# Routed experts in blocks of two halves of 64 rows, and two blocks at a time on TensorE

## The chip, the cores and the metric

The kernel runs on one core of a Trainium2 chip. The metric is the device time of one execution in microseconds (us), lower is better.

## The reference

The input `x` is 16 x 256 tokens of 256 values. It goes through two gated layers:

```
x = x + tanh(g_xattn) * cosine(LN(x) Wv^T + bv, ctx Wt^T + bt)      # attention part, per batch 256 x 256
h = LN(x)                                                           # 4096 tokens, D = 256
shared = (silu(h @ w1) * (h @ w2)) @ w3                             # one shared expert, hidden width 1024
scores = sigmoid(h @ router_w)                                      # 16 experts
top2   = top_k(scores + expert_bias, 2); gates = scores at those two, else 0
routed = sum over e of gates[:, e] * ((silu(h @ W1[e]) * (h @ W2[e])) @ W3[e])   # hidden width 256
x = x + tanh(g_ffn) * (shared + routed)
```

Each token uses two of sixteen experts, so there are 8192 routed rows. The kernel computes only those rows; how many fall to each expert is known only at run time.

## The kernel before

All five engines have a program of their own, written out by hand, and wait for each other on semaphores. The order of the work on an engine is the order of its program.

- **Attention part and router** (0 to about 118 us): eight chunks of 512 tokens. `router` (L1306) already uses strips of the array: four groups of 128 tokens go to four strips of 32 columns, `tile_position=(0, 32 * i)`, each with its own moving operand. Ahead of it on TensorE stand matmuls of line L1254 (128 elements, all 128 columns), behind it those of L1264.
- **Shared expert**, first part: steps of one chunk and one eighth of the hidden width (`hidden`, L1385, and `shared_rows`, L1406). Weights and activations are kept as sums of two f16 parts (hi and lo), so every product is three f16 matmuls: hi*hi, hi*lo, lo*hi. During these steps VectorE computes the routing, GpSimd scatters the token numbers into a table of slots, and ScalarE and VectorE cast the routed weights into `WR` (hi by L713, lo by L1076), half an expert at a time, as the list `CUTS` says per step.
- **Routed experts** (277.56 to 465.15 us): `NRUN` blocks of 128 rows. Every expert's rows are rounded up to 128, so a block belongs to one expert. Its number comes from a packed word (`blk_word`), four blocks to a word.
- **The rest of the shared expert**, in which GpSimd gathers the routed rows back (L561) and VectorE adds them (L1052); then the stores.

One routed block b goes through these steps:

1. GpSimd fetches its 128 rows by an indirect DMA into one of four slots (`fetch`, L544).
2. TensorE transposes them (`block_transpose`, L1457, two f32 transposes), into bank 2; ScalarE writes the hi part to `XTB` (`x_hi`, L749), VectorE the lo part (`x_lo`, L1131).
3. TensorE computes both hidden products (`block_hidden`, L1468, 6 matmuls of 512 elements, the weights are the moving operand).
4. ScalarE takes the silu (`r_silu`, L756), VectorE multiplies (`gated`, L1138).
5. TensorE transposes the result (`hidden_transpose`, L1477, bank 3); `g_hi` (L762) and `g_lo` (L1143) write `GT`.
6. TensorE computes the rows (`block_rows`, L1488, 6 matmuls of 256 elements, bank 4); VectorE copies them out (`rows`, L1150), SyncE stores them (`store_block`, L432).

TensorE's loop runs per b: hidden product of b, transpose of the gated part of b - 1, transpose of the rows of b + 2, rows product of b - 2. `XTB`, `GT`, `SIL`, `G` have two buffers each. `experts` reads the packed word into registers, and `weights` forms the address in `WR` from them at run time.

The functions that the diff touches:

Of the kernel before, what the change touches and what calls it, by code (L numbers as in the profile page):

```python
# [19 lines left out]
P = 128  # L20


def flamingo_block(nc, x, x_t, ctx_t, g_xattn, g_ffn, wv_t, bv, wt_t, bt, router_w, expert_bias,
# [21 lines left out]
    NRUN = (2 * TOK + E * (P - 1)) // P  # L45
    NBLK = -(-NRUN // 8) * 8
    WE = 2 * KD * RH + (RH // P) * D
# [20 lines left out]
    with ctx:  # L68
# [19 lines left out]
        XTB = sb("XTB", [P, 2, 2, KD, P], F16)  # L88
# [31 lines left out]
        blk_word = sb("blk_word", [1, NBLK // 4], I32)  # L120
        row_iota = sb("row_iota", [P, 1], F32)
        pack = sb("pack", [P, NBLK // 4], F32)
# [7 lines left out]
        def arena(shape):  # L130
# [27 lines left out]
        BV4 = XTB[:, :, :, :, :].rearrange("p a b k n -> p (a b k n)").bitcast(F32).rearrange("p (i h) -> p i h", i=TPC)  # L158
# [5 lines left out]
            .rearrange("p (a k n) -> p a k n", a=2, k=KD)  # L164

# [38 lines left out]
        ended = sb("ended", [P, E], F32)  # L204
        bef = sb("bef", [P, 1], F32)
# [4 lines left out]
        SHARED_ROWS = (bank[3], bank[4])  # L210

# [89 lines left out]
        w_lo = sem("w_lo")  # L301

# [38 lines left out]
        CUTS = [0] * (J + 2) + [2, 1, 1] * 6 + [1] * 8  # L341
# [3 lines left out]
        assert sum(TILES.values()) == NT  # L345

# [4 lines left out]
        def _(sp):  # L351
# [81 lines left out]

            with sp.Fori(0, NBLK // 4 - 1) as i:
                for u in range(4):
                    store_block(i, u)
            for b in range(NBLK - 4, NRUN):
                store_block(b // 4, b % 4)
# [18 lines left out]
        def _(pool):  # L457
# [12 lines left out]
            pool.iota(row_iota[:, :], pattern=[[0, 1]], base=0, channel_multiplier=1,  # L470
                      allow_small_or_imprecise_dtypes=True)
            pool.memset(pack[:, :], 0.0).then_inc(c_mem, 1)
            for k in range(6):

                pool.wait_ge(c_mem, 3 + k)
                pool.affine_select(out=pack[:, :], in_=pack[:, :], compare_op=ALU.not_equal, fill=float(E ** k),
                                   base=2 - k, pattern=[[-4, NBLK // 4]], channel_multiplier=1).then_inc(c_mem, 1)
# [93 lines left out]
        def _(act):  # L571
# [173 lines left out]
            def x_hi(b, u, first=False):  # L745
                act.wait_ge(b_tx, b + 1)
                if not first:
                    act.wait_ge(b_h, b - 1)
                act.activation(XTB[:, u, 0], bank[2][:, 0:KD * P].rearrange("p (k n) -> p k n", k=KD), ACT.Copy)\  # L749
                    .then_inc(b_xhi, 1)  # L750
# [7 lines left out]
            def g_hi(b, u, first=False):  # L758
# [3 lines left out]
                act.activation(GT[:, u, 0], bank[3][:, 0:RH].rearrange("p (k n) -> p k n", k=RH // P), ACT.Copy)\  # L762
                    .then_inc(b_ghi, 1)

            act.wait_ge(s_g, NSE)
            x_hi(0, 0, True)
            x_hi(1, 1, True)
            for b in range(NRUN):
                r_silu(b, b % 2, b < 2)
                if b >= 1:  # L770
                    g_hi(b - 1, (b - 1) % 2, b - 1 < 2)
                if b + 2 < NRUN:
                    x_hi(b + 2, b % 2)
            g_hi(NRUN - 1, (NRUN - 1) % 2)
# [20 lines left out]
        def _(dve):  # L795
# [190 lines left out]
            def sum_experts(inc):  # L986

                link(dve.tensor_scalar(ni[:, :], inc[:, PADT + NT - 1, :], float(P - 1), None, ALU.add))
                link(dve.tensor_scalar(bi[:, :], ni[:, :], 7, None, ALU.arith_shift_right))
# [11 lines left out]
                link(dve.tensor_scalar(base_row[:, :], nf[:, :], float(P), None, ALU.mult))  # L1001
# [21 lines left out]
            def block_experts(ends):  # L1023

                link(dve.tensor_scalar(ended[:, :], ends, row_iota[:, :], None, ALU.is_le))
                link(dve.tensor_reduce(bef[:, :], ended[:, :], AX.X, ALU.add))
                dve.tensor_scalar(bef[:, :], bef[:, :], float(E - 1), None, ALU.min).then_inc(bef_ready, 1)

            def block_words():
                dve.wait_ge(word_mm, 1)  # L1030
                dve.tensor_copy(blk_word[:, :], bank[6][0:1, 0:NBLK // 4]).then_inc(routed_ok, 1)
# [97 lines left out]
            def x_lo(b, u):  # L1129
                dve.wait_ge(b_xhi, b + 1)  # L1130
                dve.tensor_tensor(XTB[:, u, 1], bank[2][:, 0:KD * P].rearrange("p (k n) -> p k n", k=KD),  # L1131
                                  XTB[:, u, 0], ALU.subtract).then_inc(b_xlo, 1)

# [7 lines left out]
            def g_lo(b, u):  # L1141
                dve.wait_ge(b_ghi, b + 1)
                dve.tensor_tensor(GT[:, u, 1], bank[3][:, 0:RH].rearrange("p (k n) -> p k n", k=RH // P),  # L1143
                                  GT[:, u, 0], ALU.subtract).then_inc(b_glo, 1)

            def rows(b, i, u, first=False):
                dve.wait_ge(b_y, b + 1)
                if not first:
                    dve.wait_ge(st_y[u], i * 16)
                dve.tensor_copy(YS[:, u, :], bank[4][:, 0:D]).then_inc(b_yev, 1)  # L1150

            x_lo(0, 0)
            x_lo(1, 1)
            add_shared(NCA, steps=EX)
            for b in range(NRUN):
                gated(b, b % 2, b < 2)
                if b >= 1:
                    g_lo(b - 1, (b - 1) % 2)
                if b + 2 < NRUN:
                    x_lo(b + 2, b % 2)  # L1160
                if b >= 2:
                    rows(b - 2, (b - 2) // 4, (b - 2) % 4, b < 6)
            g_lo(NRUN - 1, (NRUN - 1) % 2)
            rows(NRUN - 2, (NRUN - 2) // 4, (NRUN - 2) % 4)

            dve.wait_ge(b_tg, NRUN)
            gate_hidden(NSE, NSE % J)
            hidden_lo(NSE, NSE % J)
            rows(NRUN - 1, (NRUN - 1) // 4, (NRUN - 1) % 4)


# [32 lines left out]
        def _(pe):  # L1204
# [162 lines left out]
            def words():  # L1367

                pe.wait_ge(bef_ready, 1)
                pe.matmul(bank[6][0:1, 0:NBLK // 4], bef[0:NBLK, :], pack[0:NBLK, :], start=True, stop=True)\  # L1370
                    .then_inc(word_mm, 1)
# [70 lines left out]

            def experts(i):
# [109 lines left out]
```

## Time and profile before

| | |
|---|---|
| device time, median of 3 runs | 597.67 us (597.29 to 598.88) |
| the profiled execution's own time | 600.83 us |
| its span, first to last instruction | 598.7 us |
| granted TensorE clock over the span | 0.971 |
| instructions | 11199 |
| blocks of the routed part | 79 |

In the rows further down, PE is TensorE's matmuls, PEld its weight loads (they run beside matmuls), DVE is VectorE, ACT ScalarE, POOL GpSimd, SPq the queue of SyncE. `PE bank L1468 x6` in a chain is six matmuls of line 1468. A duration of a matmul includes a fixed latency that overlaps the next one, so a stream's pace is read from starts. A row of a group has its busy time, the mean of one in ns, and the idle time of its engine ahead of it.

### The profile page before, as it was taken

The numbers are of one execution on the slowest core, as the hardware profiler recorded it, in microseconds if no ns is written. First come the engines' busy times: TensorE is split into PE (matmuls) and PEld (weight loads), VectorE is DVE, ScalarE is ACT, GpSimd is POOL, SyncE is SP. The second block draws the span as 40 slices with busy tenths as digits, with TensorE's granted clock in tenths as the row PEclk, the third lists the DMA queues.
The fourth block names the chain that finished last, engine by engine and source line by source line (L and its number), as shares of the span: only waits on it lengthen the run. The fifth ranks groups of instructions, "written<-read, shape, count | busy, mean of one in ns | idle before, by whom it ended". The sixth has DMA issues, their size and how long they took to land.

```text
span 598.7 us, 11199 instructions
## 1 busy us (share of the span) xinstructions
PE 550.9 (92%) x3410; PEld 351.6 (59%) x3410; DVE 362.7 (61%) x845; ACT 243.5 (41%) x541; POOL 273.7 (46%) x264
## 2 busy tenths in 40 slices
PE   4899899889899999598999999999999989879797
PEld 2567676555555566255666666666666555445454
DVE  2426887777877675356556556655665456454755
ACT  3435666652265554244343334333433323222322
POOL 3002675434387877733334333433340255637560
PEclk9879999999999999889999999999999999979899
DMA  8999353356151110021333333333442133624342
GB/s 236 316 376 358 125 175 142 142 194 211 36 159 36 55 37 0 2 73 37 111 114 111 107 113 117 109 107 110 111 111 78 54 108 86 193 72 133 99 138 71
DMA packets 54561, 74.25 MB, mean 124 GB/s; under 512 B 8256, under 2 KB 44544, under 8 KB 54512
## 3 DMA queue, kind: packets, MB, share of 16 engines
q1 hardware_dynamic: 44992, 52.67, 26.7%
q0 software_dynamic: 8944, 18.83, 11.9%
q10 hardware_dynamic: 576, 2.10, 1.1%
q8 instruction: 31, 0.51, 0.4%
q14 instruction: 18, 0.15, 0.1%
HBM read 50.56 MB, written 23.01 MB: 123 GB/s over the span
## 4 chain that ended last, share of the span: by engine, by line
PE 73%; DVE 11%; issue 6%; DMA 3%; POOL 3%; SPq 2%; ACT 2%; DVEq 0%; POOLq 0%; ACTq 0%
PE bank L1385 22%; PE bank L1468 17%; PE bank L1406 12%; PE bank L1488 9%; PE bank L1477 3%; PE bank L1457 3%; DMA WR<-in_ctx_t 2%; PE bank L1223 2%; POOL X L495 1%; PE bank L1250 1%; DVE STAGE L870 1%; DVE GS L1068 1%; DVE X L1040 1%; DMA xrow<-STAGE 1%; PE bank L1212 1%
## 5 line engine op out<-in xcount | busy, mean ns | idle before, releaser
L1385 PE MATMUL bank<-XTC,WS 128*128 128x512 f16 x768 | 180.3, 384 | 0.6 <-issue 0.5
L544 POOL DMA_INDIRECT ROWS<-xrow,idx x79 | 76.2, 964 | 118.9 <-PE bank L1457 113.8
L1385 PEld LDWEIGHTS bank<-XTC,WS 128*128 128x128 f16 x768 | 76.0, 99 | 81.8 <-issue 7.4
L1406 PE MATMUL bank<-WS,GS 128*128 128x256 f16 x768 | 98.5, 280 | 25.6 <-DVE GS L1068 14.0
L1468 PE MATMUL bank<-WR,XTB 128*128 x474 | 115.3, 379 | 0.6 <-issue 0.6
L1406 PEld LDWEIGHTS bank<-WS,GS 128*128 128x128 f16 x768 | 74.6, 100 | 53.8 <-DVE GS L1068 20.4
L561 POOL DMA_INDIRECT ROWS<-yrow,posi x64 | 65.4, 1021 | 67.4 <-DVE X L1052 29.6
L1062 DVE SCALAR_TENSOR_TENSOR G<-bank,SIL 128x512 f32<-128x512 f32 x63 | 43.5, 690 | 77.7 <-ACT SIL L698 57.4
L527 POOL DMA_INDIRECT slot_token<-tokid,sloti x64 | 74.6, 1165 | 23.6 <-issue 19.2
L698 ACT ACTIVATE SIL<-bank 128x512 f32<-128x512 f32 x63 | 37.6, 596 | 110.8 <-PE bank L1385 77.0
L1138 DVE SCALAR_TENSOR_TENSOR G<-bank,SIL 128x256 f32<-128x256 f32 x79 | 33.6, 425 | 76.0 <-ACT SIL L756 75.9
L756 ACT ACTIVATE SIL<-bank 128x256 f32<-128x256 f32 x79 | 30.3, 383 | 114.5 <-PE bank L1468 113.7
L1468 PEld LDWEIGHTS bank<-WR,XTB 128*128 128x128 f16 x474 | 46.2, 98 | 40.8 <-issue 2.0
L705 ACT ACTIVATE GS<-G 128x512 f16<-128x512 f32 x63 | 39.7, 630 | 63.3 <-DVE G L1062 52.7
L1488 PE MATMUL bank<-WR,GT 128*128 x474 | 64.7, 273 | 0.0
L495 POOL TENSOR_TENSOR X<-X,WR 128x512 f32 (+1 forms) x16 | 23.6, 1495 | 67.1 <-DVE WR L840 67.1
L1068 DVE TENSOR_TENSOR GS<-G,GS 128x512 f16<-128x512 f32 x56 | 38.8, 693 | 20.9 <-ACT GS L705 14.6
L1488 PEld LDWEIGHTS bank<-WR,GT 128*128 128x128 f16 x474 | 46.4, 98 | 4.7
L1143 DVE TENSOR_TENSOR GT<-bank,GT 128x256 f16<-128x256 f32 x79 | 32.8, 415 | 2.6 <-ACT GT L762 2.6
L1131 DVE TENSOR_TENSOR XTB<-bank,XTB 128x256 f16<-128x256 f32 x79 | 32.8, 415 | 1.0 <-ACT XTB L749 1.0
L1150 DVE COPY ROWS<-bank 128x256 f32<-128x256 f32 x79 | 32.8, 415 | 0.7 <-PE bank L1488 0.7
L749 ACT ACTIVATE XTB<-bank 128x256 f16<-128x256 f32 x79 | 30.9, 392 | 1.6 <-PE bank L1457 1.6
(156 smaller groups left out, 631.7 us busy)
## 6 DMA issues: line engine op xcount, KB each, us to landing
yrow<-ROWS SPq DMA_DIRECT2D x79, 128.0 KB
WR<-in_routed_w SPq DMA_DIRECT2D x39, 256.0 KB, 5.7
X<-in_x SPq DMA_DIRECT2D x4, 1024.0 KB, 12.6
xrow<-STAGE SPq DMA_DIRECT2D x8, 512.0 KB, 2.9
xtd<-STAGE SPq DMA_DIRECT2D x8, 512.0 KB, 2.6
out<-X SPq DMA_DIRECT2D x7, 512.0 KB
WR<-in_ctx_t SPq DMA_DIRECT2D x4, 768.0 KB, 10.2
WR<-in_shared_w SPq DMA_DIRECT2D x3, 1024.0 KB, 14.5
```

Of the source, the lines that this page charges most:

```text
L527: pool.indirect_dma_start(out=slot_token, in_=tokid[:, t:t + 1], in_offset=None, out_offset=bass.IndirectOffsetOnAxis(ap=sloti[:, k, t:t + ...
L544: pool.indirect_dma_start(out=XG[:, u, :], out_offset=None, in_=xrow, in_offset=bass.IndirectOffsetOnAxis(ap=idx[:, b:b + 1].bitcast(U32), ...
L561: pool.indirect_dma_start(out=YG[:, u, k, :], out_offset=None, in_=yrow, in_offset=bass.IndirectOffsetOnAxis(ap=posi[:, k, t:t + 1].bitcas ...
L698: act.activation(SIL[:, a, :], HIDDEN[a][0][:, :], ACT.Silu, scale=1.0 / WSCALE).then_inc(s_sil, 1)
L705: act.activation(GS[:, a, 0, :], G[:, a, :], ACT.Copy).then_inc(s_ghi, 1)
L1062: dve.scalar_tensor_tensor(out=G[:, a, :], in0=HIDDEN[a][1][:, :], scalar=1.0 / WSCALE, in1=SIL[:, a, :], op0=ALU.mult, op1=ALU.mult).then ...
L1068: dve.tensor_tensor(GS[:, a, 1, :], G[:, a, :], GS[:, a, 0, :], ALU.subtract).then_inc(s_glo, 1)
L1138: dve.scalar_tensor_tensor(out=G[:, u, 0:RH], in0=bank[u][:, RH:2 * RH], scalar=1.0 / WSCALE, in1=SIL[:, u, 0:RH], op0=ALU.mult, op1=ALU.m ...
L1385: last = pe.matmul(acc[:, :], WS[:, wx, at:at + P], XTC[:, u, xx, k, :], start=(k == 0 and m == 0), stop=(k == KD - 1 and m == 2))
L1406: last = pe.matmul(acc, GS[:, a, gx, i * P:(i + 1) * P], WS[:, wx, at:at + D], start=(n in (NSE, n - j) and m == 0 and i % 2 == 0), stop=( ...
L1468: last = pe.matmul(bank[u][:, :], XTB[:, u, xx, k, :], w, start=(k == 0 and m == 0), stop=(k == KD - 1 and m == 2))
L1488: last = pe.matmul(bank[4][:, 0:D], GT[:, u, gx, k, :], w, start=(k == 0 and m == 0), stop=(k == RH // P - 1 and m == 2))
```

## The change

- The rows of an expert are rounded up to 64 (`PR`), no longer to 128. A block is two halves of 64 rows that may belong to two experts. `NRUN` goes from 79 to 72, `NBLK` from 80 to 72. There is a packed word for the even halves and one for the odd ones.
- Each matmul of a block becomes two, for rows 0 to 63 and 64 to 127, on columns 0 to 63 and 64 to 127 of the array and of the output's partitions. Each first loads the 64 rows of its half into its columns of the array (a PEld instruction) and then streams its own expert's weights past them.
- TensorE reads the even half's weights from `WR` at a run-time address, as before. The odd half's are copied to fixed places `W12` and `W3` (in the staging buffer, two sets), w1 and w2 by VectorE (`odd_first`), w3 by ScalarE (`odd_second`); both read the expert's number from the packed word themselves.
- TensorE's loop takes two blocks at a time: both hidden products, both rows products of the pair before, then all transposes. Banks 5, 6 and 7 double those of the transposes and of the rows; `XTB` has four buffers.
- The casts of the weights end one step earlier.

```diff
-    NRUN = (2 * TOK + E * (P - 1)) // P
+    PARTS = 2
+    PR = P // PARTS
+    NRUN = -(-((2 * TOK + E * (PR - 1)) // PR) // PARTS)
+    NRUN += NRUN % 2
     NBLK = -(-NRUN // 8) * 8
+    NW = NBLK // 4
...
-        XTB = sb("XTB", [P, 2, 2, KD, P], F16)
+        XTB = sb("XTB", [P, 4, 2, KD, P], F16)
...
+        stage_h = stage_f.bitcast(F16)
+        W12 = stage_h[:, 0:4 * W3E].rearrange("p (u h n) -> p u h n", u=2, h=2)
+        W3 = stage_h[:, 4 * W3E:4 * WE].rearrange("p (u h n) -> p u h n", u=2, h=2)
...
+        XB = (bank[2], bank[5])
+        GB = (bank[3], bank[6])
+        YB = (bank[4], bank[7])
...
-        CUTS = [0] * (J + 2) + [2, 1, 1] * 6 + [1] * 8
+        CUTS = [0] * (J + 2) + [2, 1, 1] * 7 + [1] * 4 + [0]
...
+        def odd_half(w, b):
+            e = (w >> (4 * (b % 4 + 2))) & (E - 1)
+            return WR[:, :].rearrange("p (e h n) -> p e h n", e=E, h=2)[:, ds(e, 1), :, :]\
+                .rearrange("p a h n -> p (a h) n")
...
# ScalarE
+            def odd_second(b, w, first=False):
+                if not first:
+                    act.wait_ge(b_y, b - 1)
+                act.activation(W3[:, b % 2], odd_half(w, b)[:, :, W3E:WE], ACT.Copy).then_inc(odd_w3, 1)
...
+            for b in range(0, NRUN, 2):
+                r_silu(b, 0, b == 0)
+                r_silu(b + 1, 1, b == 0)
+                if b == 0:
+                    x_hi(2)
+                    x_hi(3)
+                if b % 4 == 0:
+                    w = act.value_load(blk_word[0:1, ds(NW + b // 4, 1)])
+                odd_second(b, w, b == 0)
+                g_hi(b, 0, b == 0)
+                g_hi(b + 1, 1, b == 0)
+                if b + 4 < NRUN:
+                    x_hi(b + 4)
+                    x_hi(b + 5)
+                odd_second(b + 1, w, b == 0)
...
# VectorE
-                link(dve.tensor_scalar(ended[:, :], ends, row_iota[:, :], None, ALU.is_le))
+                for s in range(PARTS):
+                    last = dve.tensor_scalar(ended[:, s, :], ends, row_iota[:, s:s + 1], None, ALU.is_le)
+                link(last)
...
+            def odd_first(b, w, first=False):
+                if not first:
+                    dve.wait_ge(b_h, b - 1)
+                dve.tensor_copy(W12[:, b % 2], odd_half(w, b)[:, :, 0:W3E]).then_inc(odd_w12, 1)
...
+            for b in range(0, NRUN, 2):
                 if b + 2 < NRUN:
+                    if (b + 2) % 4 == 0:
+                        w = dve.value_load(blk_word[0:1, ds(NW + (b + 2) // 4, 1)])
+                    odd_first(b + 2, w)
+                gated(b, 0, b == 0)
+                gated(b + 1, 1, b == 0)
+                if b + 2 < NRUN:
+                    odd_first(b + 3, w)
+                if b == 0:
+                    x_lo(2)
+                    x_lo(3)
+                else:
+                    rows(b - 2)
+                    rows(b - 1)
+                g_lo(b, 0)
+                g_lo(b + 1, 1)
+                if b + 4 < NRUN:
+                    x_lo(b + 4)
+                    x_lo(b + 5)
...
# TensorE, block_hidden (block_rows in the same way, with W3 and odd_w3)
+                pe.wait_ge(odd_w12, b + 1)
...
                 for k in range(KD):
-                    hi = weights(e, k * 2 * RH, 2 * RH)
-                    lo = weights(e, WE + k * 2 * RH, 2 * RH)
+                    at = k * 2 * RH
+                    hi = weights(e, at, 2 * RH), W12[:, u, 0, at:at + 2 * RH]
+                    lo = weights(e, WE + at, 2 * RH), W12[:, u, 1, at:at + 2 * RH]
                     for m, (xx, w) in enumerate(((0, hi), (0, lo), (1, hi))):
-                        last = pe.matmul(bank[u][:, :], XTB[:, u, xx, k, :], w,
-                                         start=(k == 0 and m == 0), stop=(k == KD - 1 and m == 2))
+                        for s in range(PARTS):
+                            part = slice(s * PR, (s + 1) * PR)
+                            last = pe.matmul(bank[u][part, :], XTB[:, b % 4, xx, k, part], w[s],
+                                             start=(k == 0 and m == 0), stop=(k == KD - 1 and m == 2),
+                                             tile_position=(0, s * PR))
...
-            for b in range(NRUN):
+            for b in range(0, NRUN, 2):
                 if b % 4 == 0:
                     es = experts(b // 4)
-                block_hidden(b, b % 2, es[b % 4 + 2], b < 2)
-                if b == 1:
+                block_hidden(b, es[b % 4 + 2])
+                block_hidden(b + 1, es[b % 4 + 3])
+                if b == 0:
+                    block_transpose(2)
+                    block_transpose(3)
                     pe.wait_ge(s_base, NCA + 1)
-                if b >= 1:
-                    hidden_transpose(b - 1, (b - 1) % 2, b == 1)
-                if b + 2 < NRUN:
-                    block_transpose(b + 2, (b + 2) % 4, 16 * ((b + 2) // 4 + 1))
-                if b >= 2:
-                    block_rows(b - 2, b % 2, es[b % 4], b == 2)
+                else:
+                    block_rows(b - 2, es[b % 4])
+                    block_rows(b - 1, es[b % 4 + 1])
+                hidden_transpose(b)
+                hidden_transpose(b + 1)
+                if b + 4 < NRUN:
+                    block_transpose(b + 4)
+                    block_transpose(b + 5)

             hidden(NSE, NCA % 2, EX)
-            hidden_transpose(NRUN - 1, (NRUN - 1) % 2)
-            block_rows(NRUN - 2, (NRUN - 2) % 2, es[NRUN - 2 - (NBLK - 6)])
+            block_rows(NRUN - 2, es[NRUN - 2 - LAST_WORD])
             hidden(NSE + 1, NCA % 2, EX + 1)
-            block_rows(NRUN - 1, (NRUN - 1) % 2, es[NRUN - 1 - (NBLK - 6)])
+            block_rows(NRUN - 1, es[NRUN - 1 - LAST_WORD])
```

## Rows read from the trace of the kernel before

**Rows 1.** The page: busy time per engine, and the chain that ended last.
```profile
PE 550.9 (92%) x3410; PEld 351.6 (59%) x3410; DVE 362.7 (61%) x845; ACT 243.5 (41%) x541; POOL 273.7 (46%) x264
...
PE 73%; DVE 11%; issue 6%; DMA 3%; POOL 3%; SPq 2%; ACT 2%; DVEq 0%; POOLq 0%; ACTq 0%
```

**Rows 2.** Stretches: from:to, length, busy per engine, granted clock, DMA share, GB/s.
```profile
277.56:465.15 187.59, 187.54 (x1247) 127.95 (x1248) 111.63 (x315) 73.12 (x234) 70.18 (x74) 1.00 0.36 107
```

**Rows 3.** The chain in order of time (start, us, what): first, steady and last blocks.
```profile
277.56 1.51 PE bank L1468 x6
...
455.95 1.30 PE bank L1468 x6
457.25 0.22 PE bank L1477 x2
457.47 0.22 PE bank L1457 x2
457.68 0.66 PE bank L1488 x6
458.34 1.29 PE bank L1468 x6
...
462.89 1.38 PE bank L1468 x6
...
465.15 0.86 PE bank L1385 x4
```

**Rows 4.** The timeline of ScalarE and VectorE in one steady block (start, us, what).
```profile
455.65 0.41 DVE L1143 TENSOR_TENSOR GT<-bank,GT 128x256 f16<-128x256 f32 x1
455.99 0.42 DVE L1131 TENSOR_TENSOR XTB<-bank,XTB 128x256 f16<-128x256 f32 x1
...
457.28 0.38 ACT L756 ACTIVATE SIL<-bank 128x256 f32<-128x256 f32 x1 [1.45 <-PE bank L1468]
457.56 0.38 ACT L762 ACTIVATE GT<-bank 128x256 f16<-128x256 f32 x1
```

**Rows 5.** The timeline of TensorE around one chunk's router.
```profile
77.03 1.05 PE L1254 MATMUL bank<-GS,XTB 128*128 128x128 f32 x8
78.02 0.65 PE L1306 MATMUL bank<-STAGE,rw 128*32 128x128 f32 x16
78.59 1.16 PE L1264 MATMUL bank<-ident,rt 128*128 128x128 f32 x8
```

**Rows 6.** Groups by form: TensorE's matmuls of L1254 and three weight loads.
```profile
L1254 PE MATMUL bank<-GS,XTB 128*128 128x128 f32 x64 | 9.0, 287 | 0.0
...
L1306 PEld LDWEIGHTS bank<-STAGE,rw 128*32 128x32 f32 x128 | 3.0, 109 | 3.0 <-DVE WR L840 1.5 <-issue 0.8
...
L1264 PEld LDWEIGHTS bank<-ident,rt 128*128 128x128 f32 x64 | 7.7, 189 | 1.2 <-issue 1.2
...
L1468 PEld LDWEIGHTS bank<-WR,XTB 128*128 128x128 f16 x474 | 46.2, 98 | 40.8 <-issue 2.0
```

**Rows 7.** Groups by form: VectorE, one long form and three TENSOR_SCALAR forms.
```profile
L1076 DVE SCALAR_TENSOR_TENSOR WR<-STAGE,WR 128x768 f16<-128x768 f32 x6 | 5.8, 959 | 0.2
...
L870 DVE TENSOR_SCALAR STAGE<-X,mv,rs 128x256 f32 x20 | 6.9, 409 | 1.2 <-DMA xrow<-STAGE 0.7
...
L815 DVE TENSOR_SCALAR gsum<-gsum 128x24 f32<-128x24 f32 x1 | 0.2, 178 | 0.0
...
L815 DVE TENSOR_SCALAR gsum<-gsum 128x8 f32<-128x8 f32 x1 | 0.2, 172 | 0.0
```

**Rows 8.** Groups by form: ScalarE's cast of half an expert.
```profile
L713 ACT ACTIVATE WR<-WR 128x768 f16<-128x768 f32 x26 | 20.9, 827 | 0.0
```

**Rows 9.** Groups: GpSimd's fetches of routed rows.
```profile
L544 POOL DMA_INDIRECT ROWS<-xrow,idx x79 | 76.2, 964 | 118.9 <-PE bank L1457 113.8 <-issue 3.2 <-DMA idx<-slot_token 1.8
```

**Rows 10.** The chain at 246 us; DMA queues from 280 to 460 (packets, MB, share).
```profile
246.67 5.91 issue
...
q8 instruction: 13, 0.21, 0.5%
```

More of the change, by code:

```diff
@@ L1154, in _ @@
+            odd_first(0, w, True)
+            x_lo(1)
+            odd_first(1, w, True)
             add_shared(NCA, steps=EX)
[L1155 to L1158, printed above, removed]
+            for b in range(0, NRUN, 2):
                 if b + 2 < NRUN:
-                    x_lo(b + 2, b % 2)
-                if b >= 2:
-                    rows(b - 2, (b - 2) // 4, (b - 2) % 4, b < 6)
-            g_lo(NRUN - 1, (NRUN - 1) % 2)
@@ L1450, in weights, with block_transpose @@
                     .rearrange("p a n -> p (a n)")
-            def block_transpose(b, slot, count):
-                pe.wait_ge(xg[slot], count)
-                if not (isinstance(b, int) and b == 0):
-                    pe.wait_ge(b_xlo, b)
+            def block_transpose(b):
+                slot = b % 4
+                pe.wait_ge(xg[slot], 16 * (b // 4 + 1))
+                if b >= 2:
+                    pe.wait_ge(b_xlo, b - 1)
                 for k in range(KD):
-                    last = pe.transpose(bank[2][:, k * P:(k + 1) * P], XG[:, slot, k * P:(k + 1) * P], ident[:, :])
+                    last = pe.transpose(XB[b % 2][:, k * P:(k + 1) * P], XG[:, slot, k * P:(k + 1) * P], ident[:, :])
@@ L1470, in block_hidden, with hidden_transpose @@
                 last.then_inc(b_h, 1)
-            def hidden_transpose(b, u, first=False):
+            def hidden_transpose(b):
                 pe.wait_ge(b_g, b + 1)
-                if not first:
-                    pe.wait_ge(b_glo, b)
+                if b >= 2:
+                    pe.wait_ge(b_glo, b - 1)
                 for k in range(RH // P):
-                    last = pe.transpose(bank[3][:, k * P:(k + 1) * P], G[:, u, k * P:(k + 1) * P], ident[:, :])
+                    last = pe.transpose(GB[b % 2][:, k * P:(k + 1) * P], G[:, b % 2, k * P:(k + 1) * P], ident[:, :])
@@ L1487, in block_rows @@
                     for m, (gx, w) in enumerate(((0, hi), (0, lo), (1, hi))):
-                        last = pe.matmul(bank[4][:, 0:D], GT[:, u, gx, k, :], w,
-                                         start=(k == 0 and m == 0), stop=(k == RH // P - 1 and m == 2))
+                        for s in range(PARTS):
+                            part = slice(s * PR, (s + 1) * PR)
+                            last = pe.matmul(YB[u][part, 0:D], GT[:, u, gx, k, part], w[s],
+                                             start=(k == 0 and m == 0), stop=(k == RH // P - 1 and m == 2),
+                                             tile_position=(0, s * PR))
```

110 lines of the change are left out of this document (58 added, 52 removed).

## The prediction

> **What bounds the kernel now.** I read the page's busy shares first: TensorE is busy for 92% of the span, and the chain that ended last runs through it for 73% [rows 1]. Then the stretches: the diff works on the one from the first block's first matmul (277.56) to the first matmul behind the last block (465.15), and there TensorE is busy for 187.54 of 187.59 us, VectorE for 111.6, ScalarE for 73.1 and GpSimd for 70.2, at a granted clock of 1.00 [rows 2]. Last the chain inside it: one block is hidden 1.29-1.30, transposes of G 0.22, transposes of X 0.22, row products 0.66, and the next block starts 2.39 us after the last one, with no wait between [rows 3]. Of the 79 blocks, 78 starts are (462.89 - 277.56)/78 = 2.38 us apart. So the stage is 79 blocks of TensorE work, and all else is hidden.
>
> **The change part by part.**
>
> *Fewer blocks.* 2 x 4096 routed rows padded to 64 per expert fill at most (8192 + 16 x 63)/64 = 143 halves, so 72 blocks in place of 79.
>
> *The products of a block.* Each product becomes two, on 64 columns of the array each: the hidden part issues 12 matmuls and 12 loads for 6, the rows part the same. If two halves stream side by side, the time stays at 1.29 and 0.66. The trace has such tiles: the router issues 16 matmuls of 128 elements on four strips of 32 columns, and the next group starts 0.57 us after it; the 8 untiled ones of the same size ahead of it take 0.99 up to it [rows 5]. With starts (1.05 - 0.287)/7 = 0.109 apart [rows 5, 6], 16 in series would be 1.74. So strips do overlap, four-fold, and 16 matmuls with 16 loads are issued in under 0.6 us; this block needs 24 and 24 in 1.95. I take full overlap. The bound from above is none at all: + 1.95 per block.
>
> *The price of going into tiles and out.* 8 x 0.109 = 0.87 of the 0.99 is streaming, 0.12 is left going in; 4 x 0.109 = 0.44 of the 0.57, 0.13 is left coming out [rows 5]. The new order puts H(b) H(b+1) R(b-2) R(b-1) on tiles and four transposes after them, so each pair of blocks pays one way in and one out: 0.25 us. Bounds: 0 (if the router's gaps are its own waits) and twice that.
> The Trainium skill, TensorEngine Tiling (Array Packing), § Key Properties, says that changing the tiling mode drains TensorE; it agrees with these gaps, and is the rule that speaks against the change: without it the sum below would be 9 us better.
>
> *Loads of weights.* A load of 32 f32 columns takes 109 ns, of 128 f32 189, of 128 f16 98 [rows 6]; from the first two, 0.83 ns per f32 column. Two loads of 64 columns per 107 to 109 ns of the rows part are then about 107, just hidden; the router sustains four of 32 in the same time [rows 5]. I take nothing. Bound from above: both loads in the open at 109 each, + 0.11 for each of 6 pairs, + 0.65 per block.
> The Trainium skill, same page, § Restrictions, has column tiling turn off Fast Weight Load; the 98 ns of the f16 load against 189 for f32 would be that fast form, and the sum would move only if the slower load came out from under 107 ns.
>
> *Copies of the odd expert's weights.* VectorE gains one copy of 2 x 1024 f16 per block, ScalarE one of 2 x 512. ScalarE: 768 elements took 827 ns, so 1024 take at most 1.10 us [rows 8]. Now 0.28 from start to start of its ops of 256 [rows 4]: a pair is 6 x 0.28 + 2 x 1.1 = 3.9 of 5.0 us, hidden. VectorE: its ops of 256 start 0.34 apart [rows 4], eight a pair, 2.72 us. The copy isn't in the trace. At one element per cycle it is 0.96 us for 768 plus 1280 x 1.04 ns = 2.29 us [rows 7] (the same form as the 409 ns of a TENSOR_SCALAR of 256). But the same TENSOR_SCALAR with a plain constant goes from 172 to 178 ns between 8 and 24 f32 elements, 0.4 ns for one, where one per cycle would be 17 ns more: two f32 per cycle, 8 bytes [rows 7]. At 8 bytes per cycle 2048 f16 are 512 cycles: 0.53 + 0.16 = 0.69 us. Between 0.69 and 2.29 I take 0.69, since a copy has no per-partition scalar, as the fast rows haven't. Then VectorE has 2.72 + 2 x 0.62 = 3.96 of 5.0 us. It decides once a copy takes over (5.03 - 2.72)/2 = 1.15 us.
> The Trainium skill, VectorE: DVE Perf Modes, § The perf-mode tier table, gives a bf16 copy of 2048 in SBUF 693 ns; no copy here shows it.
>
> *The order within a pair.* The waits that could bite: the copy odd_first(b+2) waits for H(b), and gated(b), both rows, both g_lo and both x_lo are queued behind it on VectorE. Followed through with T = 5.03 from the pair's start: H(b) done and seen at 1.63, odd_first to 2.3, gated(b) to 2.7; silu(b+1) to 3.3, gated(b+1) to 3.75, while the transpose of G(b+1) starts at 4.4: 0.6 spare. odd_first(b+3) to 4.4, rows to 5.0, g_lo to 5.7 (they follow ScalarE's g_hi, which waits for R(b-2) and its own copy, to 5.15), x_lo to 6.35, and the next odd_first is not due before 6.66: 0.3 spare. R(b) at T + 2.7 finds g_lo(b) 2 us old. So nothing but TensorE sets the pace. GpSimd's fetches, 0.96 each [rows 9], two in 5.0 us, are as hidden as now; the four slots and the distance in blocks are the same. Register loads of the packed word stand on ScalarE and VectorE every fourth block, inside those 0.3 and 0.6.
>
> *Ends of the stage.* The first pair has no rows products and must wait for gated(1): about 4.5 us. Then 33 pairs of 4.77 + 0.25 = 5.03 and two without X transposes of 4.59: 175.2. Sum 179.7 against 187.59: - 7.9. Behind it the tail has three more changes of tiling (+ 0.4) and one transpose pair less (- 0.2).
>
> *The rest.* One more compare, one more matmul of 18 columns, a 10% smaller table: under 0.3 us, beside the shared steps. The casts come half a step earlier, beside TensorE; the last step has none, so the first x_lo comes perhaps 0.5 us earlier; TensorE waits there for the packed word anyway: 0. After the stage all is as before, 7.7 us sooner.
> What I can't price is fetching of instructions: at 246.67 the chain has 5.91 us in which TensorE waits for nothing shown, and TensorE gets 24 instructions more a block. In the stage itself 13 instruction packets went by without such a gap [rows 10]. I take 0, and 5 us to either side, because the fetches fall at other places now.
>
> Sum for the profiled execution: its span 598.7 and 2.1 around it are 600.8; 600.8 - 7.7 = 593.1. That execution is 3.2 above the median of 597.67, so against the median: **590.0 us**.
>
> **The rivals.**
> *A, no gap at the tiles' borders, or instruction gaps that vanish.* 36 x 0.25 = 9 us less: 581. For it: the router's gaps may be its waits. Against: both times are alike to 0.01 us.
> *B, near 597: the gain eaten.* Gaps of double size (+ 9) or a VectorE copy at 1.22 us (two elements a cycle: 2.72 + 2 x 1.14 = 5.0, no slack left, each late silu shows). 595 to 600.
> *C, VectorE becomes the bound by the port that it shares with GpSimd* (slower). If a copy stands still while GpSimd writes out a fetch of 0.96 us, a pair is 2.72 + 2 x (0.62 + 0.96) = 5.9: 35 x 0.85 = + 30, so 619. For it: two fetches and two copies in each pair. Against: fetches start when the X transposes end (4.6 to 6.5), copies run from 1.6 and from 3.7; little of them meets. It decides from 0.5 us of hold-up per copy.
> The Trainium skill, SBUF — State Buffer, § Who interferes with whom, has a Vector op in a 2-port mode and GpSimd lock each other out for the whole instruction; no row here has the two together.
> *D, the copy at one element per cycle.* 2.72 + 2 x 2.2 = 7.1: + 73, so 663. For it the 409 ns row, against it the 172 and 178.
> *E, halves or loads do not overlap.* Loads in the open 0.65 x 72 = + 47, 637; nothing overlapping 1.95 x 72 = + 140, 730. Against: the router.
> *That the change does not do what it says* can't be on the count: 72 is fixed when it is built.
>
> **How the numbers follow.** About 0.3% (1.8 us) can be told from no change. Forecast 0.50 (its own range 585 to 595), A 0.10, B 0.14, C 0.14, D 0.06, E 0.06. Faster: forecast 0.49, A 0.10, B 0.03: 0.62. Same: B 0.08 and the forecast's edge 0.01: 0.09. Slower: B 0.03, C, D, E: 0.29. The range goes from A's 581 to part of C, 615; D, E and the worse half of C (0.19) are left out.
>
> **What would show it.** Hidden groups still 1.3 us for 12 matmuls; a pair of blocks 5.0 us, with two gaps of 0.12 to 0.13 around the transposes; the copy at 0.7 us; VectorE under 85% busy in the stage; ScalarE's copies at 1.0 to 1.1. Wrong would be waits on VectorE's G or on a copy in the chain (C, D), or groups of 12 that take 2.6 us (E).

## The result, and the profile after

The changed kernel takes 592.69 us (median of 4, 591.55 to 593.16) against 597.94 us (median of 4): a ratio of 0.9908, 95% interval 0.9887 to 0.9929, so 5.3 us less. Forecast were 590.0 us, with 585 to 595 as the forecast's own range. Its profiled execution took 592.25 us with a span of 590.5.

The page of the changed kernel, answering to [rows 1]:

```profile
PE 545.1 (92%) x4164; PEld 348.4 (59%) x4164; DVE 397.0 (67%) x890; ACT 305.8 (52%) x592; POOL 273.5 (46%) x257
...
PE 68%; DVE 13%; issue 8%; DMA 3%; POOL 3%; ACT 2%; another core or an unknown queue 2%; SPq 1%; DVEq 0%; POOLq 0%; ACTq 0%
```

Its stretches, answering to [rows 2]: the routed stage from the first block's first matmul to the first shared step behind it.

```profile
275.78:459.56 183.78, 181.66 (x1990) 124.45 (x1990) 145.80 (x358) 134.66 (x285) 69.81 (x67) 1.00 0.35 99
```

TensorE is still busy nearly all the time, at a clock of 1.00. VectorE went from 111.6 to 145.8 us, ScalarE from 73.1 to 134.7. The chain of a steady pair of blocks, answering to [rows 3] (L1537 is the hidden product, L1563 the rows, L1547 and L1521 the transposes of G and of X):

```profile
409.95 2.71 PE bank L1537 x24
412.66 1.31 PE bank L1563 x24
413.97 0.59 PE bank L1547 x4
414.56 0.44 PE bank L1521 x4
415.00 2.71 PE bank L1537 x24
```

24 hidden matmuls take 2.71 us and 24 rows matmuls 1.31; 12 and 12 full-width ones take 2.59 and 1.31 (the run without tiles below). So two halves stream side by side. A pair takes 5.04 to 5.05 us. Of the 0.27 above 4.77, 0.12 stands at the first hidden product (2.71 less 2.59) and 0.15 at the first transpose (0.59 less 0.44), where TensorE enters and leaves the tiles. The groups by form, answering to [rows 6 to 9]:

```profile
L563 POOL DMA_INDIRECT ROWS<-xrow,idx x72 | 76.0, 1055 | 105.8 <-PE bank L1521 92.7 <-issue 11.3 <-DMA idx<-slot_token 1.9
L788 ACT ACTIVATE STAGE<-WR 128x1024 f16 x72 | 76.8, 1066 | 10.7 <-PE bank L1563 10.1 <-issue 0.6
L1194 DVE COPY STAGE<-WR 128x2048 f16 x72 | 49.6, 689 | 17.6 <-PE bank L1537 12.6 <-issue 5.0
L1563 PEld LDWEIGHTS bank<-WR,GT 128*64 128x64 f16 x432 | 47.1, 110 | 7.9 <-issue 0.8
```

VectorE's copy takes 689 ns, ScalarE's 1066, a load of 64 columns 110, and a fetch of GpSimd now 1055 where it was 964.

**Where the 8.2 us between the two spans lie.** Same places in both chains:

| from, to | before | after | difference |
|---|---|---|---|
| start, first hidden product of the shared expert that is in the chain | 118.06 | 121.30 | +3.2 |
| ... start of the last shared rows ahead of the stage | 157.09 | 152.85 | -4.2 |
| ... first block | 2.41 | 1.63 | -0.8 |
| the routed stage | 187.59 | 183.78 | -3.8 |
| ... shared rows again | 7.22 | 7.36 | +0.1 |
| ... end | 126.33 | 123.58 | -2.8 |

The routed stage gives 3.8, not 7.9. The other large terms belong to stretches that the diff hardly touches; the experiments below say which of them are real. TensorE's very first hidden matmul of the shared expert comes earlier than the one in the chain, at 109.7 us before and 112.9 after; the text below calls it the first hidden step, and it moved by the same 3.2 us.

### The profile page after: what moved, and what is told of

Read it like the earlier page. It is cut to its first block, busy times and chain, and to the rows that moved or that the text cites. A ratio compares the mean times of both kernels' runs of the same rounds, so it can differ in the third digit from the quotient of the medians.

```text
span 590.5 us, 13102 instructions
## 1 busy us (share of the span) xinstructions
PE 545.1 (92%) x4164; PEld 348.4 (59%) x4164; DVE 397.0 (67%) x890; ACT 305.8 (52%) x592; POOL 273.5 (46%) x257
## 4 chain that ended last, share of the span: by engine, by line
PE 68%; DVE 13%; issue 8%; DMA 3%; POOL 3%; ACT 2%; another core or an unknown queue 2%; SPq 1%; DVEq 0%; POOLq 0%; ACTq 0%
PE bank L1446 18%; PE bank L1537 16%; PE bank L1467 10%; PE bank L1563 8%; PE bank L1547 3%; PE bank L1282 3%; PE bank L1521 3%; DVE X L1077 2%; DVE G L1099 2%; DMA WR<-in_ctx_t 2%; POOL X L514 2%; PE bank L1271 1%; PE bank L1309 1%; DVE GS L1105 1%
## 5 line engine op out<-in xcount | busy, mean ns | idle before, releaser
L563 POOL DMA_INDIRECT ROWS<-xrow,idx x72 | 76.0, 1055 | 105.8 <-PE bank L1521 92.7
L1467 PE MATMUL bank<-WS,GS 128*128 128x256 f16 x768 | 95.8, 275 | 22.4 <-DVE GS L1105 15.0
L1537 PE MATMUL bank<-WR,XTB 128*64 x432 | 100.1, 381 | 1.1 <-issue 0.9
L1537 PE MATMUL bank<-STAGE,XTB 128*64 128x512 f16 x432 | 100.2, 381 | 0.0
L788 ACT ACTIVATE STAGE<-WR 128x1024 f16 x72 | 76.8, 1066 | 10.7 <-PE bank L1563 10.1
L1537 PEld LDWEIGHTS bank<-WR,XTB 128*64 128x64 f16 x432 | 45.7, 109 | 42.8 <-issue 8.0
L1194 DVE COPY STAGE<-WR 128x2048 f16 x72 | 49.6, 689 | 17.6 <-PE bank L1537 12.6
L1563 PE MATMUL bank<-STAGE,GT 128*64 128x256 f16 x432 | 53.3, 273 | 0.0
L1563 PE MATMUL bank<-WR,GT 128*64 x432 | 53.3, 273 | 0.0
L1563 PEld LDWEIGHTS bank<-WR,GT 128*64 128x64 f16 x432 | 47.1, 110 | 7.9 <-issue 0.8
L1563 PEld LDWEIGHTS bank<-STAGE,GT 128*64 128x64 f16 x432 | 47.1, 110 | 0.0
```

The lines of the kernel that those rows point to most:

```text
L563: pool.indirect_dma_start(out=XG[:, u, :], out_offset=None, in_=xrow, in_offset=bass.IndirectOffsetOnAxis(ap=idx[:, b:b + 1].bitcast(U32), ...
L788: act.activation(W3[:, b % 2], odd_half(w, b)[:, :, W3E:WE], ACT.Copy).then_inc(odd_w3, 1)
L1194: dve.tensor_copy(W12[:, b % 2], odd_half(w, b)[:, :, 0:W3E]).then_inc(odd_w12, 1)
L1467: last = pe.matmul(acc, GS[:, a, gx, i * P:(i + 1) * P], WS[:, wx, at:at + D], start=(n in (NSE, n - j) and m == 0 and i % 2 == 0), stop=( ...
L1537: last = pe.matmul(bank[u][part, :], XTB[:, b % 4, xx, k, part], w[s], start=(k == 0 and m == 0), stop=(k == KD - 1 and m == 2), tile_posi ...
L1563: last = pe.matmul(YB[u][part, 0:D], GT[:, u, gx, k, part], w[s], start=(k == 0 and m == 0), stop=(k == RH // P - 1 and m == 2), tile_posi ...
```

## The experiments

The experiments were made in four series, and the kernel before takes another time in each: 575.5 us in the first (below: the quiet series), 615.9 in the second, 622.5 in the third, 637.3 in the fourth. The first and third have the same chip number, and so have the second and fourth, so the chip alone isn't shown to make the difference. In the last three series the times of one kernel spread too far for their totals to decide anything, and traces are compared. The routed stage is steadier: 187.47 to 187.59 us in the traces of the kernel before, 181.95 to 183.78 in those of the changed one.

**The changed kernel again.**

> The changed kernel once more, for a second trace of it. Theory (TensorE sets the pace of the pairs; what lies outside the routed stage varies from one execution to the next): 592.7 within 1, pairs again 5.04 to 5.06 us, stage 183.8 within 0.5; the stretch from 237 to 274 us, where the chain has gaps that nothing explains, may differ by several us. Rival (those gaps belong to the program): they stand at the same places with the same sizes within 1 us.

572.22 us (median of 10) against 575.53: ratio 0.9945, interval 0.9912 to 0.9978, so 3.3 us less. The stage is 181.95 us. The chain in the stretch of the scatters, in order of time:

```profile
241.95 1.31 PE bank L1467 x12
243.26 2.59 PE bank L1446 x12
245.85 1.31 PE bank L1467 x12
```

Steps of 3.90 without a gap, where both kernels had gaps of several us in the first comparison ([rows 10] for before). So the gaps aren't fixed by the program; what sets them is open. From the first hidden step to the routed stage the changed kernel takes 156.9 us here, 162.9 in the first comparison and 194.9 in the third series. Of the forecast for this run the total and the length of the stage (183.8 expected) were off; the pairs held, and the rival on the gaps is out. The stage came out 1.8 us shorter than in the first comparison.

**One more way out of the tiles and in.**

> The transposes of one block's rows move in between the two hidden products of the pair: the same instructions, but TensorE leaves and enters the 64-column tiles twice in a pair and not once. Theory (each way out and in costs 0.27 us together, as the traces show it): 34 pairs x 0.27 = 9 us more than the changed kernel, about 602, pairs of 5.3. Rival (the 0.27 is the latency of the transposes' own waits, not of the change of tiles): within 2 us of the changed kernel, 593.

```diff
                 block_hidden(b, es[b % 4 + 2])
+                if b >= 2 and b + 4 < NRUN:
+                    block_transpose(b + 4)
                 block_hidden(b + 1, es[b % 4 + 3])
...
                 if b + 4 < NRUN:
-                    block_transpose(b + 4)
+                    if b == 0:
+                        block_transpose(b + 4)
                     block_transpose(b + 5)
```

587.64 us, 15.4 more than the changed kernel in the same series (572.22); forecast were 9. The chain of one pair:

```profile
305.05 1.42 PE bank L1537 x12
306.47 0.39 PE bank L1521 x2
306.86 0.01 issue
306.87 1.49 PE bank L1537 x12
308.36 1.31 PE bank L1563 x24
309.67 0.59 PE bank L1547 x4
310.25 0.22 PE bank L1521 x2
```

A pair is 5.42 us, 0.38 more and not 0.27: two transposes between tiles take 0.39 where they are 0.22 among others, and the tiles are entered again for 0.20. So the border's price is real, and dearer around a short visit. 33 pairs at + 0.38 are 12.5 us of the stage's + 13.0 (194.97 against 181.95). One pair took 5.7 us: its moved transposes (415.27) waited for VectorE's `x_lo`, at the end of a chain that begins with a copy of ScalarE. Another 1.7 us of the 15.4 are in front of the stage, where this program's first hidden step comes at 114.6 us and not at 112.9. In the pair shown nothing waits at either border, so the rival (waits of the transposes) is out.

**No tiles.**

> Every block is multiplied at full width with the even half's expert alone: 6 and 6 matmuls on all 128 columns, no tiles. The copies of the odd expert's weights are still made and waited for, but not used, so the odd expert's products are left out. Theory (halves stream side by side at no cost, only the borders cost): pairs of 4.77 to 4.80 us, so 35 x 0.27 = 9.5 us less than the changed kernel, 583. Rival 1 (the loads of the halves or their streams cost as well): more than 12 us less. Rival 2 (VectorE or ScalarE is the bound as it stands, the copies hide the borders): pairs stay near 5.0, 592.

```diff
-                        for s in range(PARTS):
-                            part = slice(s * PR, (s + 1) * PR)
-                            last = pe.matmul(bank[u][part, :], XTB[:, b % 4, xx, k, part], w[s], ..., tile_position=(0, s * PR))
+                        last = pe.matmul(bank[u][:, :], XTB[:, b % 4, xx, k, :], w[0], ...)
```

562.08 us, 10.1 less than the changed kernel; the stage is 173.18 against 181.95. The chain:

```profile
341.14 2.59 PE bank L1535 x12
343.73 1.31 PE bank L1558 x12
345.04 0.44 PE bank L1544 x4
345.47 0.44 PE bank L1521 x4
345.91 2.59 PE bank L1535 x12
```

4.77 us a pair, to the hundredth what was computed from the kernel before. In a steady pair the halves cost 0.27 us and nothing else: neither loads nor streams show.

**No copies.**

> The copies of the odd expert's weights are made for the first two blocks only, so later odd halves use those weights; every matmul and every other wait stays. Theory (the copies are hidden, but for some 1.3 us at the stage's start where VectorE's chain of x_lo, copy, add, copy, gate stands on the path): 591 to 592, pairs 5.04, and GpSimd's fetches back from 1.06 to 0.96 us each if the copies hold it up through a shared port. Rival (the pace of the pairs is set by VectorE's copies or ScalarE's, with TensorE's gaps of 0.12 and 0.15 being waits for them): pairs of 4.8, 583.

```diff
-                dve.tensor_copy(W12[:, b % 2], odd_half(w, b)[:, :, 0:W3E]).then_inc(odd_w12, 1)
+                if b < 2:
+                    dve.tensor_copy(W12[:, b % 2], odd_half(w, b)[:, :, 0:W3E]).then_inc(odd_w12, 1)
...
# ScalarE's copy and TensorE's waits for both copies in the same way
```

570.69 us (median of 10), 1.5 less; the intervals of both against before overlap (0.9893 to 0.9956, and 0.9912 to 0.9978). The trace decides: pairs still 5.04 to 5.05, the stage 181.47. In the pairs the copies are hidden. At the stage's start they cost 0.47 us, not the 1.3 that was expected: the second pair begins 5.74 us behind the first, and 6.21 behind it in the changed kernel. GpSimd's fetches:

```profile
L563 POOL DMA_INDIRECT ROWS<-xrow,idx x72 | 69.3, 963 | 103.6 <-PE bank L1523 90.7 <-issue 11.3 <-DMA idx<-slot_token 1.6
```

963 ns without copies, 1093 in the changed kernel of the same series. This run takes away the copies of both engines; a steady pair of the changed kernel tells whose it is:

```profile
301.34 0.95 POOL L563 DMA_INDIRECT ROWS<-xrow,idx  x1 [2.57 <-PE bank L1521]
301.91 1.08 ACT L788 ACTIVATE STAGE<-WR 128x1024 f16 x1
302.60 1.22 POOL L563 DMA_INDIRECT ROWS<-xrow,idx  x1 [0.30 <-issue]
303.01 0.69 DVE L1194 COPY STAGE<-WR 128x2048 f16 x1 [0.35 <-PE bank L1537]
```

The fetch beside ScalarE's copy takes 0.95 us as ever, the one beside VectorE's takes 1.22. Over the stage, 35 fetches that run beside a copy of VectorE last 1199 ns in the mean, and the 32 others, all beside a copy of ScalarE, 954. VectorE's copy began in the middle of the fetch and took its usual time (694 ns in the mean beside a fetch, 684 without). So the two run at the same time, GpSimd loses some 0.25 us by it, and it has the time.

**Each copy twice.**

> VectorE makes each of its copies of the odd expert's weights twice. Theory (VectorE has 2.72 us of other starts per pair and 0.62 for a copy, TensorE 5.05): VectorE then needs 2.72 + 4 x 0.62 = 5.2, and more with its waits for the first copy's end, so it becomes the bound: pairs of 5.3 to 5.8, 9 to 26 us more than the changed kernel, 602 to 619. Rival (VectorE still has more slack than that sum says): within 2 us of 593.

Chain of this kernel, two starts of the first copy of a pair (the rows between are VectorE's and its sequencer's):

```profile
400.00 0.62 DVE STAGE L1194
...
405.31 0.62 DVE STAGE L1194
```

A pair is 5.31 us in the mean, VectorE's sum 5.2 without its waits for each first copy to end; the stage takes 193.01. So VectorE bounds now, near the point where the sum put it. The total, 611.29 us (604.30 to 636.66) against 615.9 (601.63 to 629.15), shows nothing of it.

**The kernel before with the new list of casts.**

> The kernel before, with the change's list of casts per step alone. Theory (the casts lie beside TensorE; the last step without a cast lets the first x_lo come sooner, and the first hidden product with it): 0 to 0.8 us less than before, 597 to 598, stage start 0.5 to 0.8 sooner behind the last shared rows. Rival (the 4.2 us that the changed kernel gains between 121 and 274 us come from the casts' new places): 593 to 594.

Its first hidden step starts at 109.7 us as before, its stage is 187.51 us. The stretch from there to the stage took some 14 us more than in the first comparison, so the total (621.0 against 615.9, both spread over 13 us and more) says nothing, and the rival is not tested by it. The stage's start can be read from the trace:

```profile
289.64 1.48 PE bank L1406 x12
...
L1468 PE MATMUL bank<-WR,XTB x474: 379/379/387, 291.2 to 477.5; 128*128 x158
```

From the start of the last shared rows to the first routed matmul it takes 1.6 us, against 2.41 and 2.42 in the two traces of the kernel before and 1.63 in the changed kernel. The new list of casts alone gives the 0.8 us.

**Another order at the stage's start.**

> The changed kernel with the stage's start put in another order: VectorE's first copy in the idle time before the last shared step's lo part, the third behind the first gate, the fourth behind the x_lo of blocks 2 and 3; ScalarE's first copy between the first two silus. Theory (the first pair took 6.3 us and not 4.5 because VectorE's chain stood on the path): first pair 5.0 to 5.3 us, second 5.05 to 5.3, so 1.0 to 1.6 us less than the changed kernel, 591.2 to 591.7. Rival (the start is bound by the fetches and TensorE's own waits): within 0.3 us of the changed kernel.

```diff
+                if n == NSE - 1:
+                    dve.wait_ge(routed_ok, 1)
+                    dve.wait_ge(w_lo, 2 * E)
+                    w = dve.value_load(blk_word[0:1, ds(NW, 1)])
+                    odd_first(0, w, True)
                 hidden_lo(n, n % J)
...
             x_lo(0)
-            odd_first(0, w, True)
-            x_lo(1)
             odd_first(1, w, True)
+            x_lo(1)
...
+                if b == 0:
+                    gated(0, 0, True)
+                    odd_first(2, w)
+                    gated(1, 1, True)
+                    x_lo(2)
+                    x_lo(3)
+                    odd_first(3, w)
```

The chain at the start of the changed kernel's stage (quiet series):

```profile
271.64 1.26 DVE X L1077 x3
272.90 0.60 DVE STAGE L1194
273.50 0.35 DVE G L1175 x2
...
274.08 0.68 DVE STAGE L1194
274.76 0.34 DVE XTB L1168
...
275.24 0.74 PE bank L1521 x4
...
276.00 2.78 PE bank L1537 x24
```

The second pair starts at 276.00, 6.2 us behind the first (269.8): VectorE's add, third copy, gates, fourth copy and x_lo stand one behind the other, and TensorE's last two transposes wait for them. With the new order it is 5.1 (292.6 to 297.73). Not all of the 1.1 us is the third and fourth copy: without them, the run with no copies still took 5.74, because TensorE begins block 1 only 2.0 us behind block 0, when the second copy is there; in the new order it begins 1.3 behind. But the next pair took 6.1 here:

```profile
297.73 4.12 PE bank L1547 x24
301.85 0.02 issue
301.87 0.39 ACT SIL L775
```

ScalarE's silu of block 3 starts 4.1 us behind the pair's start. The changed kernel has the same in the first comparison at 3.7, some 1.0 us after the last hidden matmul ended, and in the quiet series not at all; why ScalarE starts late there is open. The stage is 183.05 us, 0.7 less than the changed kernel's in the first comparison and 1.1 more than in the quiet series; the total is 614.0 us (594.56 to 623.62) against 615.9. So the cause of the long first pair is shown; that it can be had back as a gain is not.

**The kernel before, and the changed one, traced in one series.**

> The kernel before once more, for its trace on the chip of the three kernels below. Theory (its start runs at the full clock as in its first trace): first hidden step at 109.7 us within 0.5, routed stage 187.5 us. Rival (the start's pace differs from chip to chip): first hidden step at 113 us as in the changed kernel's traces.

> The changed kernel once more, beside a trace of the kernel before on the same chip. Theory: its start costs some 3.2 us more than before (first hidden step at 113 us against 109.7), because TensorE waits 1.4 us at the second piece of the text and then runs four groups at half the clock; the stage is 182 to 184 us against 187.5; the two together give 2.5 to 5.5 us less than before. Rival (the stage gives less and the start is alike): both at the same first step, and the same difference in the stage alone.

Before 109.8 us to the first hidden step and a stage of 187.47; the changed kernel 113.2 and 183.72. The medians are 622.5 and 623.3: the + 3.4 at the start eats most of the - 3.75 of the stage, and the gaps of this series (28.16 us in one piece in the trace of before) hide the rest:

```profile
225.33 28.16 another core or an unknown queue
```

The start of the kernels, in TensorE's timeline. The text groups, four matmuls each from the third on, wait for pieces of the text to land. Before, first comparison:

```profile
15.98 1.98 PE L1223 MATMUL bank<-WR,wt 96*128 96x512 f32 x4 [0.24 <-DMA WR<-in_ctx_t]
18.62 1.96 PE L1223 MATMUL bank<-WR,wt 96*128 96x512 f32 x4
23.40 3.02 PE L1223 MATMUL bank<-WR,wt 96*128 96x512 f32 x4 [2.04 <-DMA WR<-in_ctx_t]
```

and the changed kernel:

```profile
16.55 3.78 PE L1282 MATMUL bank<-WR,wt 96*128 96x512 f32 x4 [1.37 <-DMA WR<-in_ctx_t]
21.69 3.76 PE L1282 MATMUL bank<-WR,wt 96*128 96x512 f32 x4
26.81 3.76 PE L1282 MATMUL bank<-WR,wt 96*128 96x512 f32 x4
```

In both the third text group waits for the second piece of the text. Before, TensorE waited 0.24 us; the third and fourth group then took 1.98 and 1.96 us at the full clock, and only behind a second wait of 2.04, for the third piece, were the next two slow (3.02 and 3.62). In the changed kernel it waited 1.37 us, and all four took 3.6 to 3.8, at half; by then the third piece had landed, and the fifth group began at 26.81 in place of 23.40. The granted clock from 16 to 32 us is 0.76 and 0.51.

All fourteen traces fall into two kinds. Where the third and fourth group ran at the full clock, the first hidden step came at 109.7 to 111.5 us; where they ran at half, or fell to it within the third, it came at 112.3 to 114.6. One version of the changed kernel is of the first kind by itself, the one without copies, whose edit lies in the routed stage alone: it waited 0.58 us, had a clock of 0.78 from 16 to 32 us and its first hidden step at 110.8. So some 2 of the 3.2 us hang on the clock and not on the new code as such. The waits in front of the third group were 0.20 to 0.61 us in the first kind, leaving aside the three versions with the six matmuls described next, and 0.78 to 1.83 in the second.

Part of the longer wait can be seen in the DMA between 6.6 and 7.4 us (the last two numbers are the busy share of the DMA engines and GB/s), before and after:

```profile
6.60:7.40 0.80, 0.00 (x0) 0.00 (x0) 0.00 (x0) 0.00 (x0) 0.00 (x0) 1.00 1.04 195
6.60:7.40 0.80, 0.00 (x0) 0.00 (x1) 0.00 (x0) 0.00 (x0) 0.00 (x0) 1.00 0.16 28
```

The loading of the input nearly stands still there in all ten traces of the changed kernel and its tiled versions (20 to 47 GB/s), and neither in the three traces of before (one with the new casts) nor in the version without tiles (177 to 206 GB/s). Why is open, and it is not all: the version without tiles had its second piece at 16.02 us, as early as before, waited 0.96 us all the same because TensorE was done sooner, and fell to half the clock.

**Warm through the wait.**

> The changed kernel with six matmuls of ones in front of the third text group, so that TensorE does not stand idle for 1.4 us there; their result is not read. Theory (the half clock after that wait costs 3 us at the start): first hidden step at 110 to 111 us, granted clock of 16 to 32 us at 0.9 and more, total 2 to 3 us less than the changed kernel. Rival (the start is bound by the loads of the input, whatever the clock): first step within 0.5 us of the changed kernel's, the total the same.

```diff
             column_sums()
+            for k in range(6):
+                pe.matmul(bank[7][:, 0:P], ones[:, :], ones[:, :], start=True, stop=True)
             text(2)
```

First hidden step at 111.5 us against 113.2, the clock from 16 to 32 us 0.73 against 0.55 for the changed kernel in this series. The clock theory holds in kind; it gives 1.7 us and not 2 to 3, and the clock didn't come to the 0.9 that I had expected, because the groups behind the wait for the third piece (2.32 us) still ran at half. Total 615.86 us (606.93 to 623.28) against 623.34 (618.91 to 626.03): the spreads overlap.

**Both.**

> Both together: the six matmuls of ones and the other order at the routed stage's start (VectorE's first copy before the last shared step's lo part, with the word read one op sooner; the third copy behind the first gate; the fourth behind the x_lo of blocks 2 and 3; ScalarE's first copy between the first two silus). Theory: first pair 5.1 us against 6.2, so 1.0 to 1.3 us less than with the six matmuls alone, the fastest of all, 3 to 4 us under the changed kernel. Rival (the time saved at the start is lost in the next pair): the same as with the six matmuls alone.

> The version with the six matmuls of ones and the other start order once more, since the chip of the last comparison lost 25 to 45 us in the stretch of the scatters, more than any difference looked for. Theory (the start at the full clock gives 2 us, the first pair 1.1 us, to the changed kernel's 5 us): a ratio to before of 0.983 to 0.989 where that stretch is quiet, first hidden step at 110 to 111.5 us, first pair 5.1 us, stage 181 to 182. Rival (only the changed kernel's own gain is real): ratio 0.990 to 0.995.

First run: first hidden step 111.4, stage 183.23, 619.59 us against 622.5. It isn't the fastest of all, as was expected: the six matmuls alone have 615.86. Second, in the fourth series: 110.3, stage 183.9 (181 to 182 expected), 628.72 us (619.97 to 634.69) against 637.26 (607.69 to 656.44). As with the start order alone, the second pair is long, 6.2 and 6.3 us, which is what the rival said. In the first run TensorE waited another 1.13 us behind the six matmuls, and the third and fourth group ran at the full clock all the same. Both medians are under before and under the changed kernel where there is one, and neither has an interval; that this version is faster than the changed kernel is not shown.

## Why the prediction was right

**The mechanism and the pace of the pairs** held step by step. Halves side by side: 2.71 and 1.31 for 24 matmuls. Borders: 0.12 and 0.15, forecast 0.12 and 0.13; the run without tiles takes them away and gets 4.77, the one with another border pays 0.38. The pair was forecast at 5.03 and is 5.04 to 5.05. The copy was taken as 0.69 and is 0.689; the constant-operand rows [rows 7] were the right ones to read, not the 409 ns. ScalarE's copy was bounded by 1.10 and is 1.07. VectorE's slack was put at 0.3 and its idle time ahead of the copy is 0.3 to 0.7; with each copy doubled it sets the pace at 5.31, where the sum gives 5.2. Loads at 110 ns each stay hidden.

**The first pair** was mis-sized: 4.5 us forecast, 6.2 measured. The step counted the gate as the last thing that TensorE waits for. In fact block 1 begins 2.0 us behind block 0, when its copy is there, and behind the gate in VectorE's order stand two copies and the x_lo on which the last two transposes wait. I had followed the order within a steady pair and not within the first. Without the two later copies it is 5.74, in the new order 5.14, so 0.6 of the 1.7 us stay even then. With that one term at 6.2 the sum is 181.4, and the stage of the quiet series is 181.95. In the first comparison another 1.8 us went into a pair of 5.65 at the start, one of 5.80 from 383.81 on, in both of which ScalarE's silu came 1.0 us late, and small excesses.

**The stage's start** was put at 0 ("TensorE waits there for the packed word anyway"). It came 0.8 us sooner, and the casts' list alone does the same.

**What was not in the sum**: + 3.2 us in the first 121 us, in a part whose code the change leaves as it was. The first hidden step stands at 109.7, 109.8 and 109.7 us in the three traces with the code of before, at 112.9, 112.9 and 113.2 in those of the changed kernel. Some 2 us of it are the clock; what slows the loading of the input is open.

**How much of the hit was luck.** Start, stage's start and stage together are + 3.2 - 0.8 - 3.8 = - 1.4 us in the first comparison, where the medians differ by - 5.3. So some 4 us of that gain lie in the other stretches, and those are not the change's: from the first hidden step to the last shared rows ahead of the stage the changed kernel took 4.2 us less than before in the first comparison and 1.1 more in the third series, behind the stage 2.6 less and 2.1 more. In the quiet series, where before was not traced, the three terms make + 3.2 - 0.8 - 5.6 = - 3.2 with the times of before from its other traces, and the medians differ by - 3.3: there the account closes, and the forecast of - 7.7 is 4.4 us off. The forecast of the pairs was right for its reasons; that 590.0 came within 2.7 us of the total was in good part luck.

**The rivals.** A (no price at the borders) is refuted by the run without tiles. B came true in neither of its mechanisms, though the third series, at + 0.8 us, ended near B's number. C has a hold-up right and its victim wrong: a fetch beside VectorE's copy takes some 0.25 us longer, and the copy keeps 689 ns in the changed kernel and 684 to 694 when it is doubled. Neither waits for the whole of the other, as C supposed. D and E are refuted by the rows.

## What to carry to other kernels

Where rows padded to 128 waste whole blocks, halves of 64 on two column tiles cost 0.27 us here for each round trip between tiled and full-width work (0.38 around a visit of two transposes), so gather the tiled work and the transposes into as few groups as the buffers allow. Sum each engine's starts over one period before trusting that a copy is hidden: the sum gave both the pace and the point where VectorE takes over. Work out the first period by itself, in the order of each engine's queue, and take a wait of TensorE behind which its clock may fall as a term of its own. And when a total moves, add up the stretches that the change touches, in more than one comparison, before crediting it with the rest.

## What the runs showed that I had not expected

A wait of 1.37 us in place of 0.24 was followed by four text groups at half the clock, 3.6 to 3.8 us each, where before the first two of them had taken 2. The same program takes 157 to 195 us from its first hidden step to the routed stage. The gaps stand while GpSimd issues scatters of 4-byte elements, in the chain as "issue" or as "another core or an unknown queue", and TensorE gets little to do: 42 matmuls from 220 to 260 us in the third series' trace of before, where the changed kernel did 226 from 230 to 266 in the quiet one. That the scatters cause them is not shown. Two transposes between two tiled groups cost 0.17 + 0.20 us over their streaming, more than the 0.27 of a longer visit. And a copy of VectorE that starts during a fetch of GpSimd is not held up; the fetch grows from 0.95 to 1.22 us.
